# A layer norm, attention and gated feed-forward kernel: GpSimd's column sums in two pieces, a new order at the start, and filler matmuls on TensorE

## The chip, the cores and the metric

The kernel runs on one core of a Trainium2 chip. The metric is the device time of one execution in microseconds (us), the median of the runs. The core's engines are TensorE (PE in the profile, with PEld for its weight loads), VectorE (DVE), ScalarE (ACT), GpSimd (POOL) and SyncE (SP, which here only issues DMAs). They run side by side and wait for one another through semaphores.

## What is computed

The input x is 2048 rows of 256 numbers. It is normalized row by row, goes through causal attention with 16 heads of 128, and the result is multiplied with a gate from a small routed feed-forward layer and added to x:

```python
xn = _layernorm(x)                                   # (x - m) / sqrt(v + 1e-5), x is 2048 x 256
k, q, v = (einsum('ihd,bpd->biph', W, xn) for W in (W_K, W_Q, W_V))   # 16 heads of 128
scores = einsum('biph,biqh->biqp', k, q)             # causal mask, softmax over p with 1/sqrt(128)
z = einsum('biqp,biph->biqh', softmax(masked), v)
s = einsum('df,bqf->bqd', W_O, z_flat)
g = silu(xn @ W_base.T + b_base + 2.0 * routed_lora(xn))   # the best of 8 experts, rank 16
out = x + s * g
```

All products are float32. The kernel makes each from three TensorE passes: every operand is split into a rounded part (hi) and a remainder (lo), and hi*hi, lo*hi and hi*lo are added in PSUM.

## The kernel before

The 2048 rows are four blocks of 512 (b or g = 0 to 3), each of four tiles of 128 rows. The 16 heads are worked off in 8 pairs, and a pair has 80 steps. A step is one tile of keys (128, index kt) against a block of queries (512, index g): a Score (three matmuls), the exponentials, and some steps later a Value (three matmuls, L327 to L329). On the diagonal the tile has only 384, 256 or 128 columns.

What each engine does for a step: ScalarE first writes minus the row maxima into the score bank (the seed, L572 and L574, from `masked` or `maxrow`). TensorE adds the scores to it. ScalarE takes the exponential twice, as `probs` (L603) and rounded as `p_hi` (L604). VectorE makes `p_lo = probs - p_hi` (L662), from two operands in SBUF, and TensorE's Value needs it. GpSimd adds `probs` to `colsum` (L510 for kt = 1, L514 for later kt), one instruction a tile of up to 512 columns; these sums divide the output of a block later. ScalarE waits for the sum of tile n - 3 before it writes the `probs` of tile n + 1. GpSimd also splits weights in hi and lo (L443, L446), masks the row maxima of a diagonal (L472) and, at the start, scales blocks 1 to 3 of x (L484).

A list written by hand sets the order of all jobs: START before the first score, FIRST for pair 0, SCHEDULE for pairs 1 to 6 and LAST for pair 7. Every engine goes through the same list and takes its share of each job. The codes are: m the statistics of a block of x, n its scaling, N its transposes through TensorE (two per block), Pq and Pk the projections (digits: head of the pair, block), V the values' projection, M one tile of a head's row maxima (matmul L841, maximum on VectorE, L709 or with the mask L715), v a Value, Z, S and O the ends of a block, and | the next Score. Jobs that use an auxiliary PSUM bank share three of them in turn; TensorE waits with such a job until VectorE is through with the job three before it.

The start, in the lines that the change touches: SyncE loads x block by block, the first weights in between. VectorE takes statistics (L627, L631), adds EPS (L634), ScalarE takes the square root (L582), VectorE the reciprocal and one Newton step (L642 to L649), and scales block 0 (L655). TensorE fills the three score banks with ones (L788) and then waits for the transposes (L808). Each transposed bank is copied by ScalarE as hi (L588) and VectorE takes lo (L703). SyncE passes the row maxima of a block through DRAM to spread them over all partitions, and ScalarE reorders them into `maxrow` (L557).

## Time and profile before

| | |
|---|---|
| median of 3 runs | 1389.03 us (1389.02 to 1389.19) |
| the profiled execution | 1389.27 us |
| its span, first to last instruction | 1387.4 us |
| PE, PEld busy | 98%, 83% |
| DVE, ACT, POOL busy | 90%, 79%, 64% |
| the chain that ended last | PE 81%, DVE 13%, ACT 3%, issue 2%, POOL 1% |

The profiled execution took 1.9 us more than its span, 0.2 us more than the median. Busy times of engines overlap, so they don't add up to the span. A busy PE is not a PE at its peak: a matmul of 512 columns is shown with some 0.39 us but the next one starts earlier, so the distance between two starts tells more than a duration. The chain is followed back from the last instruction, at each step to what released it.

### The profile page before, as it was taken

To read this page: it belongs to the slowest core of one execution; us is meant where nothing else is said; L and a number is where in the kernel's file an instruction comes from. 1 tells how busy PE (TensorE), PEld (TensorE's weight loads), DVE (VectorE), ACT (ScalarE), POOL (GpSimd) and SP (SyncE) were. 2 spreads that over 40 slices of the span, in tenths; PEclk is the share of its full clock that TensorE was granted. 3 is DMA by queue.
4 is the path that set the end of the run, shared out by engine and by line. 5 is a ranking of instruction groups with operands and counts; after the bars stand their busy time and mean duration, and the time that the engine had idled before them with its cause. 6 is when DMAs were issued, how large, how long until landed. Compare 5 with 4: busy or idle time off the path is not lost.

```text
span 1387.4 us, 23197 instructions
## 1 busy us (share of the span) xinstructions
PE 1355.0 (98%) x7340; PEld 1156.6 (83%) x7340; DVE 1254.3 (90%) x2636; ACT 1100.5 (79%) x2459; POOL 892.7 (64%) x765
## 2 busy tenths in 40 slices
PE   5999999999999999999999999999999999999997
PEld 3788888888788888888888887988888888888987
DVE  6789998999899998989989999899989999889988
ACT  2688887888788897788877888788878889778675
POOL 5456784567566674666745777556766658476566
PEclk9999999999999999999999999999999999999999
DMA  3100001010100101100010000100011000010103
GB/s 99 32 16 16 16 9 46 9 17 16 31 24 9 24 8 32 31 17 8 17 39 17 16 16 8 47 9 17 15 32 24 16 17 9 23 36 16 24 9 107
DMA packets 30137, 33.74 MB, mean 24 GB/s; under 512 B 11072, under 2 KB 17728, under 8 KB 30016
## 3 DMA queue, kind: packets, MB, share of 16 engines
q1 hardware_dynamic: 30016, 32.26, 9.7%
q8 instruction: 59, 0.97, 0.3%
q14 instruction: 62, 0.51, 0.2%
HBM read 30.02 MB, written 2.23 MB: 23 GB/s over the span
## 4 chain that ended last, share of the span: by engine, by line
PE 81%; DVE 13%; ACT 3%; issue 2%; POOL 1%; DMA 0%; ACTq 0%; DVEq 0%
PE ps L327 25%; PE ps L329 24%; PE ps L328 24%; PE ps L841 7%; DVE p_lo L662 5%; DVE partmax L709 3%; PE ps L898 2%; DVE acc L751 1%; DVE z_lo L731 1%; ACT p_hi L604 1%; POOL acc L484 1%; DVE sums L735 1%; ACT ps L574 0%; ACT z_hi L609 0%; ACT probs L603 0%
## 5 line engine op out<-in xcount | busy, mean ns | idle before, releaser
L514 POOL TENSOR_TENSOR colsum<-colsum,probs 128x512 f32<-128x512 f32 (+3 forms) x512 | 640.0, 1250 | 207.9 <-ACT probs L603 176.1
L662 DVE TENSOR_TENSOR p_lo<-probs,p_hi 128x512 fp32r<-128x512 f32 (+3 forms) x640 | 576.3, 905 | 12.8 <-ACT p_hi L604 11.6
L603 ACT ACTIVATE probs<-ps 128x512 f32<-128x512 f32 (+3 forms) x640 | 345.6, 540 | 179.7 <-PE ps L329 174.8
L604 ACT ACTIVATE p_hi<-ps 128x512 fp32r<-128x512 f32 (+3 forms) x640 | 346.3, 541 | 0.0
L574 ACT ACTIVATE ps<-maxrow 128x512 f32<-128x512 f32 (+3 forms) x576 | 315.3, 547 | 0.0
L709 DVE TENSOR_REDUCE partmax<-ps 128x1 f32<-128x512 f32 x384 | 255.5, 679 | 2.7 <-PE ps L841 2.5
L327 PE MATMUL ps<-p_hi,v_hi 128*128 128x512 f32 (+3 forms) x640 | 238.0, 372 | 5.0 <-DVE p_lo L662 3.8
L327 PE MATMUL ps<-qT_hi,kT_hi 128*128 128x512 f32 (+3 forms) x640 | 237.8, 371 | 0.0
L329 PE MATMUL ps<-qT_hi,kT_lo 128*128 128x512 f32 (+3 forms) x640 | 233.0, 364 | 0.0
L328 PE MATMUL ps<-qT_lo,kT_hi 128*128 128x512 f32 (+3 forms) x640 | 232.9, 364 | 0.0
L328 PE MATMUL ps<-p_lo,v_hi 128*128 128x512 f32 (+3 forms) x640 | 232.8, 364 | 0.0
L329 PE MATMUL ps<-p_hi,v_lo 128*128 128x512 f32 (+3 forms) x640 | 232.5, 363 | 0.0
L841 PE MATMUL ps<-kT_hi,qT_hi 128*128 128x512 f32 (+3 forms) x640 | 218.5, 368 | 6.1 <-DVE qT_lo L703 2.6
L510 POOL TENSOR_TENSOR colsum<-probs 128x384 f32<-128x384 f32 (+1 forms) x64 | 79.8, 1247 | 212.2 <-ACT probs L603 212.2
L327 PEld LDWEIGHTS ps<-p_hi,v_hi 128*128 128x128 f32 x640 | 120.4, 188 | 37.5 <-DVE p_lo L662 19.4
L841 PEld LDWEIGHTS ps<-kT_hi,qT_hi 128*128 128x128 f32 x640 | 119.3, 188 | 30.1 <-DVE qT_lo L703 3.5
L327 PEld LDWEIGHTS ps<-qT_hi,kT_hi 128*128 128x128 f32 x640 | 120.6, 188 | 21.5 <-ACT ps L574 6.1
L329 PEld LDWEIGHTS ps<-qT_hi,kT_lo 128*128 128x128 f32 x640 | 120.5, 188 | 19.3
L329 PEld LDWEIGHTS ps<-p_hi,v_lo 128*128 128x128 f32 x640 | 120.4, 188 | 18.8
L328 PEld LDWEIGHTS ps<-p_lo,v_hi 128*128 128x128 f32 x640 | 120.6, 188 | 17.6
L328 PEld LDWEIGHTS ps<-qT_lo,kT_hi 128*128 128x128 f32 x640 | 120.6, 188 | 14.0
L715 DVE CUSTOM_DVE_ANT_0 ps<-ps,mask_rows 128x128 f32<-128x128 f32 (+3 forms) x256 | 124.7, 492 | 0.3
(115 smaller groups left out, 2337.2 us busy)
## 6 DMA issues: line engine op xcount, KB each, us to landing
spread<-max_dram SPq DMA_DIRECT2D x64, 256.0 KB, 3.9
wraw<-wqk_dram SPq DMA_DIRECT2D x16, 256.0 KB, 3.6
acc<-x_dram SPq DMA_DIRECT2D x4, 512.0 KB, 6.3
wraw<-wv_dram SPq DMA_DIRECT2D x8, 256.0 KB, 5.1
wraw<-wo_dram SPq DMA_DIRECT2D x8, 256.0 KB, 3.1
out_dram<-acc SPq DMA_DIRECT2D x8, 256.0 KB, 2.4
max_dram<-rowmax SPq DMA_DIRECT2D x64, 2.0 KB, 1.4
maxrow<-x_dram SPq DMA_DIRECT2D x2, 512.0 KB, 3.8
```

Source lines behind the costliest of these rows:

```text
L327: nc.tensor.matmul(dst, w_hi, m_hi, start=first, stop=False, skip_group_check=seed)
L328: nc.tensor.matmul(dst, w_hi, m_lo, start=False, stop=False, skip_group_check=seed)
L329: return nc.tensor.matmul(dst, w_lo, m_hi, start=False, stop=last, skip_group_check=seed)
L510: nc.gpsimd.tensor_tensor(total[:, c0:], before[:, c0:], tile[:, c0:], ALU.add)\
L514: nc.gpsimd.tensor_tensor(total[:, c0:], total[:, c0:], tile[:, c0:], ALU.add)\
L574: op = nc.scalar.activation(dst[:, plain:], maxrow[:, job.g, plain:], ACT.Copy)
L603: nc.scalar.activation(probs[:, k, c0:], src, ACT.Exp, scale=SCALE).then_inc(probs_ready, 1)
L604: nc.scalar.activation(p_hi[:, k, c0:], src, ACT.Exp, scale=SCALE).then_inc(hi_ready, 1)
L662: nc.vector.tensor_tensor(p_lo[:, k, c0:], probs[:, k, c0:], f32(p_hi[:, k, c0:]), ALU.subtract)\
L709: nc.vector.reduce_max(dst, src, axis=AX).then_inc(aux_free, 1)
L715: nc.vector.tensor_tensor_reduce(out=src[:, 0:w], in0=src[:, 0:w], in1=mask_rows[:, BW - w:], scale=1.0, scalar=-3.0e38, op0=ALU.add, op1= ...
L841: nc.tensor.matmul(dst[:, 0:w], qT_hi[:, job.g, job.q * P:(job.q + 1) * P], kT_hi[:, k_slot(job.head, job.c), 0:w], start=True, stop=True)\
```

## The change

Four things change.

1. GpSimd's sums (L510 and L514) of tiles with 512 or 384 columns are made in two instructions of half the columns. The semaphore rises after the second.
2. The start of the layer norm. Block 0 of x is loaded by two DMAs of two tiles each, and VectorE starts with the first. The addition of EPS (L634) is gone: ScalarE adds it inside the square root, and the Newton step takes the variance with EPS. GpSimd makes `ones_r` first and splits the first weights only when VectorE has scaled block 0. Block 1 is scaled by VectorE instead of GpSimd (`DVE_SCALED = 2`).
3. TensorE no longer waits for all constants before it fills the score banks, and issues matmuls of ones into a bank that is overwritten later: 16 before block 0's transposes, 7 before the first projection, 6 before block 1's transposes, 512 columns each.
4. START and FIRST, up to step 31 of pair 0, have another order. SCHEDULE, LAST and the rest of FIRST stay.

```diff
+                if b == 0:
+                    sp.dma_start(acc[:, 0:2, :], xt[0][:, 0:2]).then_inc(x_in_first, 16)
+                    sp.dma_start(acc[:, 2:TB, :], xt[0][:, 2:TB]).then_inc(x_in[0], 16)
+                    sp.dma_start(wraw[:, 0, :], wqk[:, 0, :]).then_inc(wqk_in, 16)
+                    continue
...
 START = (
-    "m0 n0 m1 n1 N00 N10 m2 Pk00 N01 Pq00 N11 M0020 M0000 M0010 M0030 n2 Pq01 m3 M0110 n3 N02 V01 Pk01 M0130 "
-    "M0111 M0100 M0101 M0120 M0131 "
+    "m0 n0 N00 N10 m1 m2 n1 Pq00 Pk00 N01 n2 M0010 N11 M0030 M0020 M0000 m3 n3 Pq01 V01 Pk01 M0100 N02 N12 M0131 "
+    "M0110 M0120 M0121 M0101 M0111 "
 )
...
+            nc.gpsimd.memset(ones[:, :], 1.0).then_inc(made, 1)
+            nc.gpsimd.memset(eps[:, :], EPS)
+            pool.wait_ge(made, 1)
+            nc.gpsimd.tensor_copy(ones_r[:, :], ones[:, :]).then_inc(ones_ready, 1)
...
+            pool.wait_ge(normed, 4 + TB)
             split_weights(wraw[:, 0, :], flat(wqk_hi[:, 0]), flat(wqk_lo[:, 0]), wqk_in, 16, 1, wqk_ready)
...
-                if isinstance(job, Scale) and job.b:
+                if isinstance(job, Scale) and job.b >= DVE_SCALED:
...
+            def halves(c0):
+
+                middle = (c0 + BW) // 2
+                return (slice(c0, middle), slice(middle, BW)) if c0 < BW - P else (slice(c0, BW),)
...
-                elif job.kt == 1:
-                    before = probs[:, (n - 1) % PROBS, :]
-                    nc.gpsimd.tensor_tensor(total[:, c0:], before[:, c0:], tile[:, c0:], ALU.add)\
-                      .then_inc(sum_done, 2)
                 else:
-                    pool.wait_ge(sum_done, n)
-                    nc.gpsimd.tensor_tensor(total[:, c0:], total[:, c0:], tile[:, c0:], ALU.add)\
-                      .then_inc(sum_done, 1)
+                    other = probs[:, (n - 1) % PROBS, :] if job.kt == 1 else total
+                    if job.kt > 1:
+                        pool.wait_ge(sum_done, n)
+                    for part in halves(c0):
+                        op = nc.gpsimd.tensor_tensor(total[:, part], other[:, part], tile[:, part], ALU.add)
+                    op.then_inc(sum_done, 2 if job.kt == 1 else 1)
...
-                    act.wait_ge(moments_done, job.b + 1)
-                    nc.scalar.activation(rstd[:, 1, mine], rstd[:, 0, mine], ACT.Sqrt).then_inc(sqrt_done, 1)
+                    act.wait_ge(stats_done, 2 * job.b + 2)
+                    nc.scalar.activation(rstd[:, 1, mine], moments[:, mine, 1], ACT.Sqrt, bias=eps[:, 0:1])\
+                      .then_inc(sqrt_done, 1)
...
+            def keep_busy(bank, job):
+
+                first = job.b == 0 if isinstance(job, (Normed, Project)) else False
+                if isinstance(job, Normed) and job.c == 0 and job.b < 2:
+                    times = BUSY_FIRST if first else BUSY_THIRD
+                elif isinstance(job, Project) and first and job.head == 0 and job.which == "q":
+                    times = BUSY_SECOND
+                else:
+                    return
+                for _ in range(times):
+                    nc.tensor.matmul(bank, ones_r[:, :], ones_r[:, None, :].broadcast_to([P, TB, P]), start=True,
+                                     stop=True)
```

The rows below give an engine's instructions in the order of its queue, a line for each or for several alike, with the line number in the kernel they belong to. On TensorE at the start of the program before the change, the first rows are the fill of the score banks, block 0's transposes, a projection (six matmuls), block 1's first transposes:

```order
L788 MATMUL ps<-ones_r 128x128 x12
L808 MATMUL ps<-ident,acc 128x128 x8
L327 MATMUL ps<-xT_hi,wqk_hi 128x512
L328 MATMUL ps<-xT_lo,wqk_hi 128x512
L329 MATMUL ps<-xT_hi,wqk_lo 128x512
L327 MATMUL ps<-xT_hi,wqk_hi 128x512
L328 MATMUL ps<-xT_lo,wqk_hi 128x512
L329 MATMUL ps<-xT_hi,wqk_lo 128x512
L808 MATMUL ps<-ident,acc 128x128 x4
```

The same place after the change:

```order
L805 MATMUL ps<-ones_r 128x128 x12
L821 MATMUL ps<-ones_r 128x512 x16
L841 MATMUL ps<-ident,acc 128x128 x8
L821 MATMUL ps<-ones_r 128x512 x7
L334 MATMUL ps<-xT_hi,wqk_hi 128x512
L335 MATMUL ps<-xT_lo,wqk_hi 128x512
L336 MATMUL ps<-xT_hi,wqk_lo 128x512
...
L821 MATMUL ps<-ones_r 128x512 x6
L841 MATMUL ps<-ident,acc 128x128 x4
L874 MATMUL ps<-kT_hi,qT_hi 128x256
```

Matmuls of ones now stand in three places, and both projections of block 0 (twelve matmuls, nine of them left out) come before block 1's transposes. On VectorE at the start before the change, from block 0's scaling to the first remainders of projections:

```order
L655 TENSOR_SCALAR acc<-acc,moments,rstd 128x256 x4
L627 BN_STATS stats<-acc 128x6 x4
L631 BN_AGGR moments<-stats 128x2 x4
L634 TENSOR_SCALAR rstd<-moments 128x4
L642 RECIPROCAL rstd<-rstd 128x4
L644 TENSOR_TENSOR rstd<-rstd 128x4
L646 SCALAR_TENSOR_TENSOR rstd<-rstd 128x4
L649 SCALAR_TENSOR_TENSOR rstd<-rstd 128x4
L703 TENSOR_TENSOR xT_lo<-ps,xT_hi 128x512 x2
```

The same place after the change:

```order
L673 TENSOR_SCALAR acc<-acc,moments,rstd 128x256 x4
L721 TENSOR_TENSOR xT_lo<-ps,xT_hi 128x512 x2
L648 BN_STATS stats<-acc 128x6 x4
L652 BN_AGGR moments<-stats 128x2 x4
L648 BN_STATS stats<-acc 128x6 x4
L652 BN_AGGR moments<-stats 128x2 x4
L660 RECIPROCAL rstd<-rstd 128x4
L662 SCALAR_TENSOR_TENSOR rstd<-rstd 128x4
L664 SCALAR_TENSOR_TENSOR rstd<-moments,rstd 128x4
L667 SCALAR_TENSOR_TENSOR rstd<-rstd 128x4
L673 TENSOR_SCALAR acc<-acc,moments,rstd 128x256 x4
```

Block 0's transposed remainders (L703, now L721) come right after its scaling, ahead of the statistics of blocks 1 and 2, and block 1's scaling is now here. On GpSimd, in the first steps of pair 0 before the change:

```order
L514 TENSOR_TENSOR colsum<-colsum,probs 128x256
L514 TENSOR_TENSOR colsum<-colsum,probs 128x128
L510 TENSOR_TENSOR colsum<-probs 128x512
L514 TENSOR_TENSOR colsum<-colsum,probs 128x512
L443 TENSOR_TENSOR wo_hi<-wraw,zeros 128x512
L446 TENSOR_TENSOR wo_lo<-wraw,wo_hi 128x512
```

The same place after the change:

```order
L531 TENSOR_TENSOR colsum<-colsum,probs 128x128 x3
L531 TENSOR_TENSOR colsum<-probs 128x256 x2
L531 TENSOR_TENSOR colsum<-colsum,probs 128x256 x2
L453 TENSOR_TENSOR wo_hi<-wraw,zeros 128x512
L456 TENSOR_TENSOR wo_lo<-wraw,wo_hi 128x512
```

A tile of 512 columns is now two instructions of 256 (and one of 256 columns two of 128); the weights' splits are whole as before.

## Rows read from the trace of the kernel before

**Rows 1.** The profile's page, its first line.

```profile
span 1387.4 us, 23197 instructions
```

**Rows 2.** Busy time by stretch: length; PE, PEld, DVE, ACT, POOL busy; PEclk; DMA.

```profile
0.00:60.00 60.00, 40.62 (x181) 31.32 (x182) 42.29 (x126) 25.82 (x54) 27.13 (x43) 0.97 0.22 66
31.50:35.00 3.50, 2.97 (x14) 2.97 (x15) 0.86 (x3) 0.96 (x3) 3.50 (x4) 0.51 0.16 57
60.00:1383.00 1323.00, 1314.33 (x7161) 1125.26 (x7160) 1210.12 (x2509) 1074.70 (x2407) 865.52 (x723) 1.00 0.09 22
```

**Rows 3.** The chain that ended last, its start: start us, us, what.

```profile
6.55 1.25 DVE rstd L634
...
8.87 3.04 DVE acc L655 x4
```

**Rows 4.** Timeline of the start: start us, us, instruction, [idle before <-releaser].

```profile
2.81 2.82 PE L788 MATMUL ps<-ones_r 128*128 128x128 f32 x12 [2.81 <-POOL ones_r L463]
...
16.23 0.76 PE L327 MATMUL ps<-xT_hi,wqk_hi 128*128 128x512 f32 x1 [2.93 <-DVE xT_lo L703]
...
16.79 0.63 PE L328 MATMUL ps<-xT_lo,wqk_hi 128*128 128x512 f32 x1
17.21 0.63 PE L329 MATMUL ps<-xT_hi,wqk_lo 128*128 128x512 f32 x1
...
27.14 9.65 POOL L484 TENSOR_SCALAR acc<-acc,moments,rstd 128x256 f32<-128x256 f32 x8 [7.32 <-DVE rstd L649]
...
38.26 0.64 POOL L472 TENSOR_SCALAR_AFFINE_SELECT gates<-maxrow 128x512 f32<-128x512 f32 x1 [1.47 <-ACT maxrow L557]
...
39.80 0.46 PE L327 MATMUL ps<-qT_hi,kT_hi 128*128 128x512 f32 x1
```

**Rows 5.** Groups of the first 40 us: busy us, mean ns | idle before.

```profile
L627 DVE BATCH_NORM_STATS2 stats<-acc 128x6 f32<-128x256 f32 x16 | 5.6, 410 | 4.7 <-DMA acc<-x_dram 4.7
...
L703 DVE TENSOR_TENSOR xT_lo<-ps,xT_hi 128x512 fp32r<-128x512 f32 x5 | 3.3, 685 | 2.0 <-ACT xT_hi L588 2.0
...
L715 DVE CUSTOM_DVE_ANT_0 ps<-ps,mask_rows 128x128 f32<-128x128 f32 (+3 forms) x6 | 2.6, 459 | 0.0
```

**Rows 6.** Line L655, VectorE's scaling of block 0: ns min/median/max.

```profile
L655 DVE TENSOR_SCALAR acc<-acc,moments,rstd x4: 400/728/1420, 8.9 to 11.5; 128x256 f32<-128x256 f32 x4
```

**Rows 7.** Waits from 60 to 1387 us: us in total, times, longest.

```profile
PEld ps L327 <- DVE p_lo L662: 19.4, 39, 0.8
```

**Rows 8.** Timeline around one such wait, in pair 1.

```profile
309.57 1.30 POOL L514 TENSOR_TENSOR colsum<-colsum,probs 128x512 f32<-128x512 f32 x1 [0.81 <-ACT probs L603]
...
309.71 1.70 DVE L662 TENSOR_TENSOR p_lo<-probs,p_hi 128x512 fp32r<-128x512 f32 x1
...
312.39 1.30 POOL L446 TENSOR_TENSOR wqk_lo<-wraw,wqk_hi 128x512 fp32r<-128x512 f32 x1
...
312.54 1.70 DVE L662 TENSOR_TENSOR p_lo<-probs,p_hi 128x512 fp32r<-128x512 f32 x1
...
313.64 1.74 POOL L514 TENSOR_TENSOR colsum<-colsum,probs 128x512 f32<-128x512 f32 x1
...
313.85 0.34 PE L329 MATMUL ps<-qT_hi,kT_lo 128*128 128x384 f32 x1
...
314.29 0.50 PE L327 MATMUL ps<-p_hi,v_hi 128*128 128x512 f32 x1
...
314.63 0.40 PE L328 MATMUL ps<-p_lo,v_hi 128*128 128x512 f32 x1
...
314.86 0.40 PE L329 MATMUL ps<-p_hi,v_lo 128*128 128x512 f32 x1
```

**Rows 9.** Groups by shape, 60 to 1387 us, `p_lo` of full tiles: busy, mean.

```profile
L662 DVE TENSOR_TENSOR p_lo<-probs,p_hi 128x512 fp32r<-128x512 f32 x445 | 462.8, 1042 | 12.4 <-ACT p_hi L604 11.6
```

**Rows 10.** Timeline: a sum of 256 columns, and a `p_lo` beside an idle GpSimd.

```profile
49.27 0.73 POOL L514 TENSOR_TENSOR colsum<-colsum,probs 128x256 f32<-128x256 f32 x1
...
300.11 0.66 DVE L662 TENSOR_TENSOR p_lo<-probs,p_hi 128x512 fp32r<-128x512 f32 x1
```

More of the change, by code:

```diff
@@ L38 @@
 X_FIRST = 56
+DVE_SCALED = 2
+BUSY_FIRST, BUSY_SECOND, BUSY_THIRD = 16, 7, 6
 LORA_STEP = 49
@@ L237, in attention_layer @@
         rank = sb("rank", [P, TB, E])
+        eps = sb("eps", [P, 1])
         warm = sb("warm", [P, 2])
@@ L315, in attention_layer, with normed_until @@
         assert mask_at == sorted(mask_at) and max_blocks == sorted(max_blocks)
+        def normed_until(b):
+            return 4 * b + TB * min(b, DVE_SCALED)
         def columns(t):
@@ L449, in flat @@
                 return t.rearrange("p a b -> p (a b)") if len(t.shape) == 3 else t.rearrange("p a b c -> p (a b c)")
+            nc.gpsimd.memset(ones[:, :], 1.0).then_inc(made, 1)
+            nc.gpsimd.memset(eps[:, :], EPS)
+            pool.wait_ge(made, 1)
+            nc.gpsimd.tensor_copy(ones_r[:, :], ones[:, :]).then_inc(ones_ready, 1)
             nc.gpsimd.memset(ident[:, :], 0.0).then_inc(made, 1)
             nc.gpsimd.memset(mask_rows[:, :], 0.0).then_inc(made, 1)
-            nc.gpsimd.memset(zeros[:, :], 0.0)
-            nc.gpsimd.memset(ones[:, :], 1.0).then_inc(made, 1)
+            nc.gpsimd.memset(zeros[:, :], 0.0).then_inc(made, 1)
             for e in range(E):
                 nc.gpsimd.memset(rank[:, :, e:e + 1], float(E - e))
-            pool.wait_ge(made, 3)
+            pool.wait_ge(made, 4)
             diagonal = dict(compare_op=ALU.not_equal, base=0, pattern=[[-1, P]], channel_multiplier=1)
@@ L461, in _ @@
             nc.gpsimd.affine_select(out=mask_rows[:, BW - P:], in_=mask_rows[:, BW - P:], compare_op=ALU.is_ge,
-                                    fill=MASKED, base=0, pattern=[[-1, P]], channel_multiplier=1)
-            nc.gpsimd.tensor_copy(ones_r[:, :], ones[:, :]).then_inc(consts, 1)
+                                    fill=MASKED, base=0, pattern=[[-1, P]], channel_multiplier=1).then_inc(consts, 1)
+            pool.wait_ge(normed, 4 + TB)
             split_weights(wraw[:, 0, :], flat(wqk_hi[:, 0]), flat(wqk_lo[:, 0]), wqk_in, 16, 1, wqk_ready)
@@ L632, in block_moments @@
                 op.then_inc(stats_done, 1)
-                dve.wait_ge(stats_done, 2 * b + 2)
-                nc.vector.tensor_scalar(rstd[:, 0, TB * b:TB * (b + 1)], moments[:, TB * b:TB * (b + 1), 1], EPS, None,
-                                        ALU.add).then_inc(moments_done, 1)
             def scale_block(b):
-                mine, done = slice(TB * b, TB * (b + 1)), TB * (b > 0) + 4 * b
-                r, v = rstd[:, 2, mine], rstd[:, 0, mine]
+                mine, done = slice(TB * b, TB * (b + 1)), normed_until(b)
+                r, v = rstd[:, 2, mine], moments[:, mine, 1]
                 dve.wait_ge(sqrt_done, b + 1)
@@ L643, in scale_block @@
                 dve.wait_ge(normed, done + 1)
-                nc.vector.tensor_tensor(rstd[:, 3, mine], r, r, ALU.mult).then_inc(normed, 1)
+                nc.vector.scalar_tensor_tensor(rstd[:, 3, mine], r, -0.5, r, ALU.mult, ALU.mult).then_inc(normed, 1)
                 dve.wait_ge(normed, done + 2)
-                nc.vector.scalar_tensor_tensor(rstd[:, 4, mine], rstd[:, 3, mine], -0.5, v, ALU.mult, ALU.mult)\
+                nc.vector.scalar_tensor_tensor(rstd[:, 4, mine], v, EPS, rstd[:, 3, mine], ALU.add, ALU.mult)\
                   .then_inc(normed, 1)
@@ L650, in scale_block @@
                   .then_inc(normed, 1)
-                if b:
+                if b >= DVE_SCALED:
                     return
                 dve.wait_ge(normed, done + 4)
-                for t in range(TB):
+                for t in range(TB * b, TB * (b + 1)):
                     nc.vector.tensor_scalar(acc[:, t, :], acc[:, t, :], moments[:, t, 0:1], rstd[:, 5, t:t + 1],
@@ L782, in _ @@
         def _(pe):
-            pe.wait_ge(consts, 1)
+            pe.wait_ge(ones_ready, 1)
             for bank in st:
@@ L800, in _ @@
                         pe.wait_ge(aux_free, job.aux - AUX_BANKS + 1)
+                    keep_busy(dst, job)
+                    if job.aux == 0:
+                        pe.wait_ge(consts, 1)
                 if isinstance(job, Normed):
@@ L803, in _ @@
                         tok = TB * job.b + t
-                        if job.b == 0:
-                            pe.wait_ge(normed, 4 + t + 1)
+                        if job.b < DVE_SCALED:
+                            pe.wait_ge(normed, normed_until(job.b) + 4 + t + 1)
                         else:
-                            pe.wait_ge(scaled, TB * (job.b - 1) + t + 1)
+                            pe.wait_ge(scaled, TB * (job.b - DVE_SCALED) + t + 1)
                         op = nc.tensor.transpose(dst[:, t * P:(t + 1) * P],
```

15 lines of the change are left out of this document (8 added, 7 removed), and 20 rows, old and new, of the table FIRST.

## The prediction, made before the changed kernel ran

> **What bounds the kernel now.** I read the span first, then the engines by stretch, then the chain and the waits. The span is 1387.4 us [rows 1]. From 60 us to 1383 us TensorE is busy 1314 of 1323 us, VectorE 1210 of them and GpSimd 866; in the first 60 us TensorE is busy only 40.6 [rows 2]. The TensorE work of the whole program doesn't change except for the ones, so a gain can come from three places only: the 19.4 us without a matmul in the first 60 us, the time there at half clock, and the small holes in the dense part.
>
> *The start.* Block 0's statistics begin when x has landed, at 4.7 us [rows 5]. The EPS addition on 4 columns takes 1.25 us and the scaling of four tiles 3.04 us, done at 11.9 [rows 3], though a tile takes 0.40 us when nothing is in its way [rows 6]. The first projection starts at 16.23 and the first score at 39.80 [rows 4]. Ahead of the score GpSimd scales blocks 2 and 3, eight tiles in 9.65 us from 27.14 on, then masks the maxima (38.26), and 1.54 us after the mask's start the score runs [rows 4].
>
> *The clock.* Projections of 512 columns start 0.42 us apart at 17 us [rows 4], which is TensorE's lower level (1.2 GHz); at 314 us it is 0.23 us, near the upper one [rows 8]. Between 31.5 and 35 us, after stretches of waiting, the granted clock is 0.51 [rows 2].
>
> *The dense part.* TensorE waits for `p_lo` 39 times [rows 7]. One such wait: the matmul before it has 384 columns and starts at 313.85, the next one at 314.29, 0.44 us later instead of about 0.17 (384/512 of 0.23); the one behind starts 0.34 us later instead of 0.23 [rows 8]. That is 0.38 us lost. Why `p_lo` is late is in the same rows: GpSimd adds a tile from 309.57 to 310.87, and the `p_lo` that starts at 309.71 takes 1.70 us and ends at 311.41, 0.54 us after GpSimd. Beside an idle GpSimd it takes 0.66 us [rows 10]; the mean is 1.04 us over 445 [rows 9]. So VectorE waits for the end of GpSimd's instruction, and that costs it (1.04 - 0.66) x 445 = 169 us in all.
>
> By the Trainium skill, page "SBUF — State Buffer", section "SBUF: two separate sides", VectorE with two SBUF inputs and GpSimd share a port pair that is locked for a whole instruction, and the loser blocks fully. The trace agrees: 0.54 us after GpSimd's end.
>
> **The change, part by part.**
>
> *Block 0's norm (sum's first term).* The EPS addition goes (1.25 us). With the weights' split behind the scaling, four tiles cost 0.40 + 3 x 0.32 = 1.4 us instead of 3.04 (0.32 being what a tile adds in the queue; I work it out from the four statistics, 5.6/4 = 1.4 us a block [rows 5], which run alike). The first half of x lets two of the four statistics run early; the same bytes have to land for the second half, so I take 0.7 us, half of the 1.4 (bounds 0 and 1.4). 11.9 - 1.25 - 1.6 - 0.7 = 8.3 us. The square root with a bias I take like the one without. Then ScalarE's copy (0.6 us, as VectorE's of 0.685 [rows 5]) and the remainders of two banks, 2 x 0.64: block 0 is in place at about 10.8. The split of the first weights, now from 8.3 on, takes at most 2 x 1.3 us (both halves like that of [rows 8]) and ends by 10.9, level with it. First projection at 10.8 instead of 16.2: **5.4 us**.
>
> *The ones.* The fill takes 2.82 us from 2.81 on [rows 4] and moves ahead by some 1.3 us, since only one memset and one copy stand before it. So 16 matmuls start near 4.3: at 0.42 us they end at 11.0, at 0.23 us at 8.0. The tiles are scaled from 7.3 on. When the clock rises is the open point: between 31.5 and 35 us it was down for the whole 3.5 us with 2.97 us of work in them [rows 2], and came back at the end. The same from 1.5 us on gives 5, and the ones end near 8.4. The transposes then take 0.15 us each at full clock and the evacuation is about in time: cost 0 to 0.5 us. The groups of 7 and 6 (1.6 and 1.4 us at full clock) lie in waits for `xT_lo` and for block 1's scaling; without that cover they would cost 3 us together. Their return is that the projections, 24 matmuls before the first score, run at 0.23 us instead of 0.42, partly off the path.
>
> *From the first projection to the first score.* After, VectorE sets the pace up to block 3's numbers: three blocks' statistics and small operations (3 x 2.6 us; 2.6 is what block 0 needs from 4.7 to 8.87 without the 1.25 and ScalarE's turn of 0.3), the scaling of block 1 (1.4), four remainders (2.8), four masked maxima (4 x (0.46 + 0.14) = 2.4) and a row maximum, 0.2: 14.6 us, from 10.8 to 25.4, with small gaps 25.8. GpSimd gets block 2 at about 19.7 and is through at 24.5, waits, takes block 3 in half of 9.65 us: 30.6. Then mask and seed, 1.54: first score at 32.2. TensorE's own list of auxiliary jobs comes to 32.5, by VectorE's maxima. That is 39.8 - 32.5 = **7.3 us** for the start as a whole (the 5.4 included), and one transposed bank more is done by then (4 transposes, 0.5 us). Block 1's scaling costs GpSimd 4.8 us less and VectorE 1.4 more. I keep 7.5, with 4 and 10 as bounds: 4 if the ones run to 11 us, 10 if the first steps of pair 0 close their holes too.
>
> *GpSimd's pieces.* A sum of 256 columns takes 0.73 us [rows 10], so a tile takes 1.46 instead of 1.30: some 400 tiles x 0.16 = 64 us more for GpSimd, which has 457 us idle in the dense part [rows 2]. That hides it; without this cover the path would carry it. A `p_lo` that asks during the first piece now waits for 0.73 us at most, and saves 1.30 - 0.73 = 0.57 us; 0.73/1.30 = 56% of those that meet a sum do. Some of the blockers are splits and masks, which stay whole (the second `p_lo` of [rows 8] waits for one). I expect 0.18 us off the mean of 1.04, 80 us less for VectorE. For TensorE the lateness counts: 39 waits x 0.38 = 15 us, and each hole is smaller than the 0.57 us of a single saving. With three in four gone that is **11 us**; bounds 0 (other work of VectorE sets the wait) and 19 (all of them, and the waits for maxima behind the same queue).
>
> Does VectorE get in between two pieces at all? They are issued back to back. [rows 8] show it: GpSimd's sum has started at 313.64, before its split's end at 313.69, yet the waiting `p_lo` ends at 314.24 and the sum takes 1.74. So the waiting engine comes next.
>
> **Sum.** 1389.0 - 7.5 - 11 = **1370.5 us** for the median (the profiled execution is 0.2 us above it, its span 1.9 below).
>
> **The rivals.**
>
> *A: the pieces bring nothing.* The waits have another cause: the 39 are set by VectorE's total (1210 of 1323 us), and SCHEDULE, made for whole sums, finds new places to wait. For it: [rows 8], where the last blocker is a split. Against: VectorE's total itself falls. 1381.5 us.
>
> *B: the start brings little.* The ones run at half clock until 11 us, or the aux banks hold TensorE up, and pair 0 gives back. Gain 1 to 4 there: 1375 to 1379 us.
>
> *C, the other side: GpSimd falls behind.* Between its pieces it is blocked by `p_lo` (0.54 us): a tile costs 0.73 + 0.54 + 0.73 = 2.0 us, and a step lasts (1383 - 60)/620 = 2.1 us. With splits of 2.6 us in between, the sum of tile n - 3 comes late, ScalarE holds the exponential, TensorE the score. It decides from the point where GpSimd's work per step passes 2.1 us for longer than three steps. Price: 2 us a pair for 8 pairs and no gain of 11, 1389 - 7.5 + 16 = 1397.5 us. Against it: 457 us of idle time [rows 2], and that only about half of the tiles can block both ways.
>
> *D: GpSimd keeps the port pair over both pieces*, which would make a `p_lo` wait 1.46 us; 39 holes of 0.16 more, 1388 us. [rows 8] speak against it, though with a split and a sum, not two pieces.
>
> **How the numbers follow.** Both gains as worked out 0.70, A 0.12, B 0.09, C 0.05, D 0.04. Lower end: start 10 and pieces 17 give 1362; upper end: A, at 1382. What a measurement here can tell from no change is 0.2%, 2.8 us, so faster means below 1386.2. Faster 0.91 (the first three), same 0.04 (D), slower 0.05 (C).
>
> **What would show it.** First projection near 10.8 us and first score near 32.5; a granted clock of 1.00 from about 7 us to the end of the dense part; `p_lo` of 512 columns with a mean near 0.86 us; fewer than 15 waits of TensorE for `p_lo`; GpSimd's busy time near 960 to 1050 us. C would show as waits of ScalarE's `probs` for the sums, A as the same 39 waits at a shorter `p_lo`, D as `p_lo` of up to 2.0 us. The prediction fails if the pieces meet fewer `p_lo` than I think, or if the start's new order leaves TensorE waiting behind the first scores.

## The result, and the profile after

| | before | after |
|---|---|---|
| median | 1389.11 us (1389.02 to 1389.51, 4 runs) | 1380.99 us (1380.36 to 1381.24, 4 runs) |
| span of the profiled execution | 1387.4 us | 1379.1 us |

The ratio is 0.9936 with a 95% interval of 0.9924 to 0.9949 (the two medians of the table divide to 0.9942, inside it). The kernel is 8.1 us faster; 18.5 were forecast. The time lies 0.8% above the forecast.

The profile's page of the changed kernel, its first lines (answers to the busy times in the table ahead):

```profile
span 1379.1 us, 23750 instructions
PE 1358.0 (98%) x7369; PEld 1164.6 (84%) x7369; DVE 1180.9 (86%) x2636; ACT 1100.0 (80%) x2459; POOL 1011.0 (73%) x1274
```

GpSimd's 1011 us lie in the forecast 960 to 1050, but they are 118 more than before (893 us), where the prediction's sum had 64. The sums of full tiles before (60 to 1387 us), and then their pieces after (60 to 1379 us), tell why:

```profile
L514 POOL TENSOR_TENSOR colsum<-colsum,probs 128x512 f32<-128x512 f32 x336 | 502.9, 1497 | 150.4 <-ACT probs L603 130.7 <-POOL colsum L514 0.4
```

```profile
L531 POOL TENSOR_TENSOR colsum<-colsum,probs 128x256 f32<-128x256 f32 x669 | 592.1, 905 | 84.4 <-ACT probs L621 55.0 <-POOL colsum L531 0.9
```

A tile took 1.50 us on average and takes 1.81, two pieces of 905 ns: 0.31 us more, where the durations of an undisturbed GpSimd (0.73 and 1.30 us) gave 0.16. Each piece is lengthened by 0.17 us, nearly as much as a whole sum by its 0.20. The `p_lo` of 512 columns alone, in the same groups with the forms apart (60 to 1370 us), answers to [rows 9]:

```profile
L680 DVE TENSOR_TENSOR p_lo<-probs,p_hi 128x512 fp32r<-128x512 f32 x444 | 391.7, 885 | 23.1 <-ACT p_hi L622 22.8
```

1042 ns became 885. And the waits of 60 to 1379 us (in total, times, longest), which answer to [rows 7]:

```profile
PEld ps L334 <- DVE p_lo L680: 11.4, 23, 1.3
...
ACT ps L589 <- POOL gates L485: 3.1, 1, 3.1
PE ps L334 <- ACT ps L591: 2.8, 1, 2.8
```

TensorE's weight loads wait 23 times for `p_lo` instead of 39, 11.4 us instead of 19.4. The last two lines are new: one wait of ScalarE for a mask of GpSimd, and behind it one of TensorE for the seed. Windows of the same trace, to be read beside [rows 2] (behind the five engines stand PEclk, the DMA share and GB/s):

```profile
0.00:60.00 60.00, 54.45 (x252) 43.49 (x253) 43.49 (x136) 30.63 (x64) 27.62 (x48) 0.91 0.23 67
19.90:26.70 6.80, 6.56 (x21) 5.33 (x22) 5.03 (x24) 2.43 (x5) 6.11 (x6) 0.50 0.13 39
60.00:1375.00 1315.00, 1303.52 (x7119) 1121.15 (x7117) 1135.89 (x2499) 1069.35 (x2396) 983.37 (x1227) 1.00 0.09 22
204.20:207.60 3.40, 3.40 (x16) 3.40 (x15) 0.00 (x0) 1.45 (x4) 0.46 (x1) 0.50 0.69 168
```

The clock is at its lower level (0.50, 1.2 GHz) for 6.8 us from 19.9 on, for 3.4 us from 33.5 on, and again for 3.4 us at 204, right behind the new wait. The start, from the timeline, one row for each landmark:

```profile
3.44 1.40 DVE L648 BATCH_NORM_STATS2 stats<-acc 128x6 f32<-128x256 f32 x4 [3.44 <-DMA acc<-x_dram]
...
6.42 1.39 DVE L673 TENSOR_SCALAR acc<-acc,moments,rstd 128x256 f32<-128x256 f32 x4
...
3.96 4.93 PE L821 MATMUL ps<-ones_r 128*128 128x512 f32 x16
...
11.43 0.47 PE L334 MATMUL ps<-xT_hi,wqk_hi 128*128 128x512 f32 x1
...
22.04 0.63 PE L336 MATMUL ps<-xT_hi,wqk_lo 128*128 128x512 f32 x1
22.46 0.63 PE L334 MATMUL ps<-xT_hi,wqk_hi 128*128 128x512 f32 x1
...
24.88 4.82 POOL L502 TENSOR_SCALAR acc<-acc,moments,rstd 128x256 f32<-128x256 f32 x4 [0.69 <-DVE rstd L667]
31.90 0.64 POOL L485 TENSOR_SCALAR_AFFINE_SELECT gates<-maxrow 128x512 f32<-128x512 f32 x1 [2.20 <-ACT maxrow L574]
...
33.61 0.63 PE L334 MATMUL ps<-qT_hi,kT_hi 128*128 128x512 f32 x1
...
35.13 0.60 ACT L621 ACTIVATE probs<-ps 128x512 f32<-128x512 f32 x1 [1.27 <-PE ps L336]
```

The first score starts at 33.61 instead of 39.80 [rows 4], 6.2 us earlier. The first exponential starts at 35.13 instead of 40.75, only 5.6 earlier, because this score runs at the lower clock (0.63 us a matmul, as the rows at 22 us, which are 0.42 us apart).

**Where the rest went.** The first exponential of a pair is a mark that every trace has, since a pair is 80 steps in all kernels here. For pair 2, before and then after:

```profile
373.71 0.60 ACT L603 ACTIVATE probs<-ps 128x512 f32<-128x512 f32 x1 [0.22 <-PE ps L329]
...
538.42 0.60 ACT L603 ACTIVATE probs<-ps 128x512 f32<-128x512 f32 x1 [0.22 <-PE ps L329]
```

```profile
369.13 0.60 ACT L621 ACTIVATE probs<-ps 128x512 f32<-128x512 f32 x1 [0.21 <-PE ps L336]
...
532.24 0.60 ACT L621 ACTIVATE probs<-ps 128x512 f32<-128x512 f32 x1 [0.21 <-PE ps L336]
```

Pair 2 took 164.71 us and takes 163.11. I read all pairs so, from the timeline of each kernel's trace (us; the last pair goes to the end of the span):

| kernel | first exp. | 0 | 1 | 2 | 3 | 4 | 5 | 6 | 7 | after first exp. |
|---|---|---|---|---|---|---|---|---|---|---|
| before | 40.8 | 168.0 | 165.0 | 164.7 | 164.8 | 164.7 | 162.5 | 164.8 | 192.3 | 1346.7 |
| after | 35.1 | 169.3 | 164.8 | 163.1 | 163.1 | 163.2 | 163.2 | 163.1 | 194.2 | 1343.9 |
| e1_pieces | 40.8 | 170.2 | 164.4 | 163.2 | 163.2 | 163.2 | 163.1 | 163.2 | 194.5 | 1344.9 |
| e2_start | 33.7 | 166.3 | 164.9 | 164.7 | 164.6 | 164.7 | 164.7 | 164.6 | 192.4 | 1347.0 |
| e6_one_mask | 35.6 | 165.7 | 163.3 | 163.2 | 163.2 | 163.3 | 163.2 | 163.1 | 194.3 | 1339.4 |
| e8_both | 35.1 | 166.0 | 163.3 | 163.2 | 163.2 | 163.3 | 163.2 | 163.2 | 192.4 | 1337.9 |
| e12_splits | 33.9 | 165.2 | 162.9 | 162.7 | 162.8 | 162.9 | 162.7 | 162.7 | 191.8 | 1333.6 |

After against before: 5.6 us from the first exponential, 1.6 in each of pairs 2, 3, 4 and 6, 0.3 in pair 1; against that 1.3 lost in pair 0, 0.7 in pair 5 and 1.9 in pair 7. Together that is 8.4 us, the difference of the spans but for rounding.

**The hole in pair 0.** GpSimd, then ScalarE, then TensorE in the timeline near the end of pair 0:

```profile
186.64 15.27 POOL L531 TENSOR_TENSOR colsum<-colsum,probs 128x256 f32<-128x256 f32 x16
201.87 0.63 POOL L485 TENSOR_SCALAR_AFFINE_SELECT gates<-maxrow 128x512 f32<-128x512 f32 x1
...
197.10 1.15 ACT L574 ACTIVATE maxrow<-spread 128x512 f32<-128x512 f32 x1
...
202.62 0.28 ACT L589 ACTIVATE ps<-gates 128x128 f32<-128x128 f32 x1 [3.09 <-POOL gates L485]
...
200.15 0.40 PE L874 MATMUL ps<-kT_hi,qT_hi 128*128 128x512 f32 x1
203.36 0.50 PE L334 MATMUL ps<-qT_hi,kT_hi 128*128 128x512 f32 x1 [2.81 <-ACT ps L591]
```

and ScalarE and GpSimd in the same place before:

```profile
204.38 1.15 ACT L557 ACTIVATE maxrow<-spread 128x512 f32<-128x512 f32 x1
...
191.91 13.76 POOL L514 TENSOR_TENSOR colsum<-colsum,probs 128x512 f32<-128x512 f32 x8
205.67 0.64 POOL L472 TENSOR_SCALAR_AFFINE_SELECT gates<-maxrow 128x512 f32<-128x512 f32 x1
```

The maxima are ready at 198.25 (197.10 + 1.15), but the mask stands behind eight tiles of sums that GpSimd works off without a gap, and starts at 201.87. Eight tiles take 15.27 us in pieces and took 13.76 whole, 1.91 against 1.72 each.

Only half of the lateness of 3.6 us comes from GpSimd. Counted from the first exponential, the mask starts 1.8 us later than before (166.74 against 164.92 us): 1.5 from these eight tiles and 0.3 from those before them. The maxima are ready 1.7 us earlier (163.12 against 164.78), since the rest of pair 0 got shorter. And before there was no slack: the maxima were ready at 205.53 and the mask started at 205.67. So GpSimd had to keep pace with a faster chain, and became slower. The steps are shorter there than the average of 2.1 us, as ScalarE's exponentials of the first and the last of the eight tiles show:

```profile
183.89 0.63 ACT L621 ACTIVATE probs<-ps 128x512 f32<-128x512 f32 x1
...
196.14 0.49 ACT L621 ACTIVATE probs<-ps 128x384 f32<-128x384 f32 x1 [0.45 <-PE ps L336]
```

That is 1.75 us a step for sums of 1.91; before it was 1.82 (190.70 to 203.42) for sums of 1.72. The seed waits, TensorE stands for 2.81 us, and the clock drops behind it for 3.4 us, in which TensorE does half of what it could: some 1.7 us more, by that estimate.

### The profile page after: what moved, and what is told of

Its sections match the earlier page's. It is cut to its first block, busy times and chain, and to the rows that moved or that the text cites. A ratio compares the mean times of both kernels' runs of the same rounds, so it can differ in the third digit from the quotient of the medians.

```text
span 1379.1 us, 23750 instructions
## 1 busy us (share of the span) xinstructions
PE 1358.0 (98%) x7369; PEld 1164.6 (84%) x7369; DVE 1180.9 (86%) x2636; ACT 1100.0 (80%) x2459; POOL 1011.0 (73%) x1274
## 4 chain that ended last, share of the span: by engine, by line
PE 84%; DVE 9%; POOL 3%; ACT 1%; issue 1%; POOLq 0%; DVEq 0%; ACTq 0%
PE ps L334 25%; PE ps L336 24%; PE ps L335 24%; PE ps L874 8%; DVE p_lo L680 3%; POOL colsum L531 3%; DVE partmax L727 2%; PE ps L931 2%; DVE v_lo L721 1%; DVE z_lo L749 1%; DVE sums L753 0%; ACT v_hi L606 0%; PE ps L821 0%; ACT p_hi L622 0%; ACT ps L591 0%
## 5 line engine op out<-in xcount | busy, mean ns | idle before, releaser
L531 POOL TENSOR_TENSOR colsum<-colsum,probs 128x256 f32<-128x256 f32 (+2 forms) x960 | 751.2, 801 | 126.3 <-ACT probs L621 79.5
L680 DVE TENSOR_TENSOR p_lo<-probs,p_hi 128x512 fp32r<-128x512 f32 (+3 forms) x640 | 499.3, 784 | 25.8 <-ACT p_hi L622 25.2
L531 POOL TENSOR_TENSOR colsum<-probs 128x256 f32<-128x256 f32 (+1 forms) x128 | 100.8, 809 | 184.8 <-ACT probs L621 184.8
L334 PEld LDWEIGHTS ps<-p_hi,v_hi 128*128 128x128 f32 x640 | 120.5, 188 | 29.6 <-DVE p_lo L680 11.4
```

The costliest lines, as they stand in the source:

```text
L334: nc.tensor.matmul(dst, w_hi, m_hi, start=first, stop=False, skip_group_check=seed)
L531: op = nc.gpsimd.tensor_tensor(total[:, part], other[:, part], tile[:, part], ALU.add)
L680: nc.vector.tensor_tensor(p_lo[:, k, c0:], probs[:, k, c0:], f32(p_hi[:, k, c0:]), ALU.subtract)\
```

## The experiments

Each kernel is compared with the kernel before on the same chip. e1 to e4 ran together, then e5 to e8, then e9 to e12; the kernel before took 1388.52, 1388.54 and 1389.69 us beside them. All compute everything that the changed kernel computes.

**e1_pieces**: the kernel before, with GpSimd's two pieces alone.

```diff
...
+                    for part in halves(c0):
+                        op = nc.gpsimd.tensor_tensor(total[:, part], other[:, part], tile[:, part], ALU.add)
+                    op.then_inc(sum_done, 2 if job.kt == 1 else 1)
```

As in the changed kernel, `halves` makes two pieces of a tile of 256 columns too, and leaves only those of 128 whole.

> The kernel before with GpSimd's sums in two pieces and nothing else of the change. Theory 1 (the pieces shorten TensorE's waits for p_lo by some 1.6 us a pair in six of eight pairs, and lose part of it again where GpSimd's queue falls behind, above all at the last steps of pair 0, where a mask stands behind a row of sums): 1389.1 - 6 x 1.65 + a hole of 1 to 5 us, 1380 to 1384 us, and a wait of ScalarE for the mask near 210 us. Rival A (the pieces bring nothing, all of the gain is the start's): 1388 to 1390 us. The changed kernel itself is 1381.0.

Measured: 1387.05 us, ratio 0.9988 (0.9978 to 0.9998). Alone the pieces bring next to nothing in the total, yet its pairs 2 to 4 and 6 take 163.2 us as in the changed kernel. The hole is there too, with the same 3.1 us, in the waits and in GpSimd's timeline:

```profile
ACT ps L576 <- POOL gates L472: 3.1, 1, 3.1
...
192.96 15.28 POOL L518 TENSOR_TENSOR colsum<-colsum,probs 128x256 f32<-128x256 f32 x16
208.19 0.63 POOL L472 TENSOR_SCALAR_AFFINE_SELECT gates<-maxrow 128x512 f32<-128x512 f32 x1
```

So the hole comes with the pieces and not with the new start. Pair 0 is 2.2 us longer than before, and pair 7 too.

**e2_start**: the changed kernel with whole sums.

```diff
-                return (slice(c0, middle), slice(middle, BW)) if c0 < BW - P else (slice(c0, BW),)
+                return (slice(c0, BW),)
```

> The changed kernel with GpSimd's sums whole again, so only the start, the ones and the new order. Theory 1: the start is worth 5.6 to 7 us at step 72 of pair 0, and without the pieces there is no late mask: 1382 to 1383.5 us, first exponential at 35.1 us, TensorE's waits for p_lo again near 39. Rival A: 1381 us, like the changed kernel. Rival B (the start brings little): above 1386 us.

Measured: 1384.41 us, ratio 0.9969 (0.9958 to 0.998). That is 4.1 us less than the kernel before took beside it. The first exponential starts at 33.7, 1.4 us before the changed kernel's; but the profiled execution, at 1382.67 us, is the fastest of the seven. There is no hole at the end of pair 0, and the waits for `p_lo` are back (60 to 1380 us):

```profile
PEld ps L334 <- DVE p_lo L680: 21.9, 44, 0.8
```

The clock was at its lower level for one stretch only, 3.4 us from 21.0 on. A window in it:

```profile
21.10:24.30 3.20, 2.91 (x8) 2.17 (x8) 3.02 (x17) 0.08 (x1) 3.20 (x4) 0.50 0.02 1
```

Up to the first score the program is the same in both, so the start's gain varies with where the clock falls. Pair 5 takes 164.7 us here, with whole sums, like its neighbours.

**e3_mask**: every mask two steps earlier in GpSimd's queue.

```diff
-            mask_at.append(max(order_at[block], diagonal - MASK_AHEAD))
+            mask_at.append(max(order_at[block] - 2, diagonal - MASK_AHEAD))
```

> The changed kernel, but where the mask's place in GpSimd's queue is set by ScalarE's reordering of the maxima, it stands two sums earlier. Theory 1 (the 3.2 us hole at 200 us, and the half clock of some 3.4 us behind it, come from the mask queued behind sums that are late): the hole goes, 5 us less, 1375 to 1377 us, and the granted clock stays at 1.00 at 204 us. Rival (the hole comes from the maxima's way through DRAM or from ScalarE, and the mask's place is of no matter): 1380.5 to 1381.5 us, with the hole where it was.

Measured: 1394.7 us, ratio 1.0043 (1.0028 to 1.0058): slower than before. The hole of pair 0 is gone (165.3 us), but pairs 2, 3, 5 and 6 take 166.8. Its waits from 60 us on show why:

```profile
POOL gates L485 <- ACT maxrow L574: 41.9, 20, 3.9
PE ps L931 <- POOL colsum L531: 13.1, 7, 2.2
```

GpSimd now stands at masks whose maxima aren't there (41.9 us instead of the changed kernel's 8.9), and TensorE waits seven times for the last sum of a block. Behind four of these waits, at 458, 625, 956 and 1124 us, the granted clock is at its lower level for 3.4 us; they lie in the four pairs of 166.8 us, while pairs 1 and 4 take 165.5 and 165.3. A queue in order takes a step that comes too early as badly as one too late.

**e4_order**: the changed kernel with START and FIRST of before.

```diff
-    "m0 n0 N00 N10 m1 m2 n1 Pq00 Pk00 N01 n2 M0010 N11 M0030 M0020 M0000 m3 n3 Pq01 V01 Pk01 M0100 N02 N12 M0131 "
+    "m0 n0 m1 n1 N00 N10 m2 Pk00 N01 Pq00 N11 M0020 M0000 M0010 M0030 n2 Pq01 m3 M0110 n3 N02 V01 Pk01 M0130 "
...
```

> The changed kernel with START and FIRST of the kernel before (pieces, ones, and the new layer norm stay). If the new order carries the start's gain: 1386 us or more, with the first score near 38 us. If the faster layer norm alone carries it: 1381 to 1383 us, with the first score near 36 us. The late mask at the end of pair 0 depends on how far GpSimd is behind there, and should stay, since the last steps of pair 0 are the same in both orders.

Measured: 1389.55 us, ratio 1.0005 (0.9996 to 1.0014). The first exponential starts at 43.4, later than before. The first projection, in the timeline:

```profile
15.42 0.76 PE L334 MATMUL ps<-xT_hi,wqk_hi 128*128 128x512 f32 x1 [4.54 <-DVE xT_lo L721]
```

In the old order VectorE does block 1's statistics and scaling (m1, n1) before it takes block 0's remainders, and TensorE stands 4.5 us; and blocks 2 and 3 are again scaled in one row of eight tiles, from 28.4 to 38.0. The faster layer norm brought nothing in this order. Why the first exponential is even 2.6 us later isn't settled: the granted clock is lower from 32.5 to 39.3 us and from 42.7 on, where the kernel before has one such stretch, from 31.6 to 35.0.

**e5_no_ones**: the changed kernel without the matmuls of ones.

```diff
-BUSY_FIRST, BUSY_SECOND, BUSY_THIRD = 16, 7, 6
+BUSY_FIRST, BUSY_SECOND, BUSY_THIRD = 0, 0, 0
```

> The changed kernel without the 29 matmuls of ones. Theory 1 (they lie in TensorE's waits and only keep its clock up): the projections and transposes before the first score run at 0.43 us a matmul of 512 columns up to about 15 us, first exponential 1 to 3 us later, 1382 to 1384 us. If they only delay: 1379 to 1381 us. If they make no difference: 1381 us.

Measured: 1378.88 us, ratio 0.993 (0.9916 to 0.9945), the same as with them. In the timeline its first projections stand 0.43 us apart, at the lower clock, where the changed kernel's run at the upper one, but they start earlier:

```profile
10.73 0.76 PE L334 MATMUL ps<-xT_hi,wqk_hi 128*128 128x512 f32 x1 [1.50 <-DVE xT_lo L721]
11.29 0.63 PE L335 MATMUL ps<-xT_lo,wqk_hi 128*128 128x512 f32 x1
11.72 0.63 PE L336 MATMUL ps<-xT_hi,wqk_lo 128*128 128x512 f32 x1
```

The granted clock reads 1.00 in the profile here (a window from 11 to 16 us), which 0.43 us a matmul doesn't fit; at the start I go by the distance. 10.73 against 11.43: here the ones cost 0.7 us and give back as much. The first exponential starts at 34.7 instead of 35.1. But 11.43 is near the best of the traces with ones and the new order, in which the first projection starts between 11.39 (e8) and 12.77 us (e6); without ones it is 10.73 and 10.74 (e9). So the ones cost 0.7 to 2.0 us.

**e6_one_mask**: one mask alone two steps earlier, the one of the hole.

```diff
-            mask_at.append(max(order_at[block], diagonal - MASK_AHEAD))
+            mask_at.append(max(order_at[block] - 2 * (gi == 2 * NB), diagonal - MASK_AHEAD))
```

> The changed kernel with the mask two sums earlier at one place only, the first block of pair 1, whose mask is the one that came 3.1 us late at 200 us. In the last round the earlier mask at every block mended pair 0 (165.3 us from its first exponential to pair 1's instead of 169.3) but made pairs 2 to 7 longer (166.8 us instead of 163.1), with TensorE waiting for sums. Theory 1 (a single late mask costs 4 us in pair 0 and 1.6 us of half clock in pair 1, and nothing else is wrong): pair 0 165.3, pair 1 163.1, pairs 2 to 6 163.1 each; ratio to the changed kernel's own time 0.996, so about 0.990 of the kernel before. Rival (the hole moves to the next mask or sum): no less than the changed kernel, 0.993 to 0.994.

Measured: 1376.89 us, ratio 0.9909 (0.9892 to 0.9925). GpSimd in the same place:

```profile
186.66 11.73 POOL L531 TENSOR_TENSOR colsum<-colsum,probs 128x256 f32<-128x256 f32 x12
198.41 0.64 POOL L485 TENSOR_SCALAR_AFFINE_SELECT gates<-maxrow 128x512 f32<-128x512 f32 x1
```

The mask starts at 198.41, when the maxima are just ready (198.27 here), the clock stays up there, pair 0 takes 165.7 instead of 169.3 and pair 1 163.3 instead of 164.8. This one place had cost 4.9 us.

**e8_both**: e6, and whole sums in pair 7.

```diff
...
-                return (slice(c0, middle), slice(middle, BW)) if c0 < BW - P else (slice(c0, BW),)
+                return (slice(c0, middle), slice(middle, BW)) if c0 < BW - P and n < (PAIRS - 1) * TILES else (slice(c0, BW),)
...
```

> As the one with a single earlier mask, and in pair 7 the sums are whole again. With pieces pair 7 took 194.2 us from its first exponential to the end, with whole sums 192.4. Theory 1 (each loss is GpSimd's queue being late, at known places): 1.8 us below the kernel with the single earlier mask, 0.9885 of the kernel before. If pair 7's loss is not GpSimd's queue but something of the start: no difference between the two.

Measured: 1374.94 us, ratio 0.9897 (0.9882 to 0.9912). The intervals of e6 and e8 overlap, so the totals alone don't tell them apart, but pair 7 takes 192.4 as before, instead of 194.3. In it the output's work comes on top for GpSimd, which is busy for 139 us of it in the changed kernel and for 126 of the pairs before it. So the pieces cause the loss. Where it arises is known in part only: TensorE stands 0.4 us for a split of the weights that e8 doesn't wait for, and 1.1 us for the last `p_lo` instead of 0.6.

**e7_quarters**: four pieces of 128 columns.

```diff
-                middle = (c0 + BW) // 2
-                return (slice(c0, middle), slice(middle, BW)) if c0 < BW - P else (slice(c0, BW),)
+                return [slice(c, c + P) for c in range(c0, BW, P)]
```

> The changed kernel with every sum in pieces of 128 columns (four for a full tile). Theory 1 (p_lo waits for the end of one GpSimd instruction, and GpSimd pays a fixed part and a blocking for each piece): mean p_lo of full tiles falls from 0.88 to about 0.75 us, a tile costs GpSimd 4 x 0.46 = 1.84 us plus blocking, about the 2.04 us of a step, so it falls behind: TensorE and ScalarE wait for sums and masks, pairs of 166 us or more, 1400 us or more in all. If the fixed part of a piece can be hidden: pairs of 162 to 163 us.

Measured: 1436.57 us, one run. Now GpSimd keeps up in no pair: all take 170 us or more. The waits for it in the dense part:

```profile
ACT probs L620 <- POOL colsum L530: 53.6, 59, 2.1
ACT ps L588 <- POOL gates L485: 27.8, 13, 5.3
```

This is rival C as it was written: ScalarE's `probs` wait for the sums 59 times.

**e9_both_no_ones**: e8 without the ones.

```diff
-BUSY_FIRST, BUSY_SECOND, BUSY_THIRD = 16, 7, 6
+BUSY_FIRST, BUSY_SECOND, BUSY_THIRD = 0, 0, 0
```

> The best kernel so far (the change, one earlier mask, whole sums in pair 7) without the matmuls of ones. In the last round the first exponential came at 34.7 us without ones and at 35.1 to 35.6 with them, so I expect no difference that can be measured: 0.9885 to 0.990 of the kernel before. If the ones do pay in most executions, and that profile was a lucky one: 0.991 to 0.992.

Measured: 1373.12 us, ratio 0.9885 (0.987 to 0.99), against e8's 0.9897: again no effect of the ones that can be told apart.

**e10_old_start**: e1 with the two mends of e8, so the pieces without the start.

```diff
...
-                return (slice(c0, middle), slice(middle, BW)) if c0 < BW - P else (slice(c0, BW),)
+                return (slice(c0, middle), slice(middle, BW)) if c0 < BW - P and n < (PAIRS - 1) * TILES else (slice(c0, BW),)
...
-            mask_at.append(max(order_at[block], diagonal - MASK_AHEAD))
+            mask_at.append(max(order_at[block] - 2 * (gi == 2 * NB), diagonal - MASK_AHEAD))
```

> The kernel before with only the sums in pieces in pairs 0 to 6, one earlier mask and whole sums in pair 7: the steady part alone, with the old start. Theory 1 (pieces are worth 1.6 us in each of pairs 1, 2, 3, 4 and 6 and as much or a little more in pair 0, once their backlog is mended; nothing in pairs 5 and 7): first exponential at 40.8, 1389 - 9.5 = 1379.5 us, 0.993 of the kernel before. If the pieces need the new start: 0.996 or more.

Measured: 1380.9 us, ratio 0.9935 (0.9923 to 0.9948). Its first exponential starts at 38.7, and from there to the end it takes 1337.9 us, 8.8 less than before. e8 takes the same 1337.9. So mended pieces are worth 8.8 us, and that adds to the start's gain.

The first exponential at 38.7 is 2.1 us earlier than in the kernel before, though all code up to it is the same. The first projection starts at 14.19 instead of 16.23. VectorE's timeline has the reason:

```profile
6.42 0.17 DVE L638 TENSOR_SCALAR rstd<-moments 128x4 f32<-128x4 f32 x1
...
8.16 1.38 DVE L659 TENSOR_SCALAR acc<-acc,moments,rstd 128x256 f32<-128x256 f32 x4
```

The EPS addition takes 0.17 us instead of 1.25 and the scaling 1.38 instead of 3.04 [rows 3]. Here both start ahead of GpSimd's next split of weights (at 6.45 and 9.27 us); in the kernel before they start just behind it (6.50 and 8.73). Which comes first differs between traces of the same code (in e1 the addition takes 1.25 us, as in the kernel before), so part of what the new start takes away is lost in some executions only.

**e12_splits**: e8, and the weights' splits in two pieces each too.

```diff
...
+                for part in parts:
+                    op = nc.gpsimd.tensor_tensor(hi[:, part], raw[:, part], zeros[:, 0:1].broadcast_to([P, w]), ALU.add)
+                op.then_inc(weight_hi, 1)
...
+                for part in parts:
+                    op = nc.gpsimd.tensor_tensor(lo[:, part], raw[:, part], f32(hi[:, part]), ALU.subtract)
+                op.then_inc(ready, 1)
```

> The best kernel so far with the weights' splits on GpSimd in two pieces each as well. Theory 1 (what is left of TensorE's waits for p_lo comes behind whole splits): four splits a pair, each p_lo of 1.8 us behind one falls to about 1.2, pairs 1 to 6 fall from 163.2 to 162.5 us, 0.5% ahead at most 4 us in all: 0.986 to 0.989 of the kernel before. If GpSimd's added time costs as much: pairs of 163.2 us or more, 0.990 or more.

Measured: 1370.13 us, ratio 0.9865 (0.9852 to 0.9878), the fastest version of all, 1.35% below the kernel before. Every pair is 0.3 to 0.8 us shorter than e8's, with fewer waits for `p_lo` (e8: 11.2 us, 24 times):

```profile
PEld ps L334 <- DVE p_lo L685: 7.4, 18, 0.8
```

**e11_again**: the changed kernel once more, with no edit.

> The changed kernel itself, to stand beside the others of this call on one chip: 0.9936 of the kernel before again (interval before 0.9924 to 0.9949), first exponential at 34 to 35.5 us by where the clock falls, the late mask at 200 us again.

Measured: 1380.93 us, ratio 0.9935 (0.9922 to 0.9947). The result stands, and e9, e10 and e12 can be read against it, as they ran beside it.

## Why the prediction was too high in its gain

**Block 0's norm: right.** The first half of x let the statistics start at 3.44. The square root takes 0.30 us with its bias, the scaling 1.39 (1.4 forecast), and it ended at 7.81 against 8.3. The first projection came at 11.43 against 10.8, so the 5.4 us measured 4.8. The ones ended at 8.9, and transposes and remainders followed from there; the terms as the prediction writes them out add up to 10.2 and hold no transposes. The 16.2 it counts from is not firm either, as e10 shows with 14.2.

**First projection to first score: 0.5 us too good**, which with those 0.6 makes the first score 1.1 us late (33.6 against 32.5). Block 2 was scaled from 19.36 on (19.7 forecast), block 3 done at 29.70 (30.6 forecast): VectorE's and GpSimd's shares were right. What failed is "a granted clock of 1.00 from about 7 us": from 19.9 to 26.7 and from 33.5 on it was 0.50. Six projections and twelve matmuls of V ran there, and everything behind them came later: the mask stood 2.20 us for the maxima. The start term of 7.5 us measured 5.6 here. In all kernels with this start and order the first exponential came between 32.4 (e9) and 35.6 (e6), and the granted clock goes with it: 32.4 where it never fell once it had risen, 33.7 to 33.9 in the four with one low stretch ahead of it (e2, e3, e7, e12), 34.7 to 35.6 in the five with a second one from about 33 us on. With the old start it came between 38.7 (e10) and 40.8, so the start gives 3.1 to 8.4 us. By medians it gives 4.1 alone (e2) and 4.8 beside mended pieces (13.6 in e8, 8.8 in e10). When the clock falls there stays open, and it differs between executions of one kernel (19.9 us in the changed kernel's trace, 22.3 in e11's).

**The ones: cost 0.7 to 2.0 instead of 0 to 0.5, and no return in total.** They raised the clock before the first projection, and delayed it; the ratios are 0.9936 with them and 0.993 without (e5), 0.9897 and 0.9885 (e8, e9). The forecast had the lower level end with them, and no new one begin.

**The pieces in the regular pairs: right in mechanism, near in size.** 11 us over 8 pairs is 1.4 a pair; pairs 2, 3, 4 and 6 gave 1.6. VectorE fell by 74 us in the dense part (1210 of 1323 us to 1136 of 1315; 80 forecast), `p_lo` to 885 ns (860). The count of waits was wrong: 23 instead of fewer than 15, with less than half of the lost time gone. e12 shows what sets part of the rest: GpSimd's splits, which stayed whole. Pair 5 gave nothing, as it had taken 162.5 us before already. That is not a property of whole sums, since it takes 164.7 in e2; why it was short in that trace is open.

**The step that failed** is "which has 457 us idle in the dense part [rows 2]. That hides it". It is a sum over 1323 us. At the end of pair 0 GpSimd has no gap for eight tiles, and each took 0.19 us more, while the maxima came 1.7 us earlier. So the mask behind them, which had been just in time, was late by 3.6 us. That, the clock behind it and the loss in pair 7 took 4.9 + 1.9 us (e6 and e8 show both by mending them), so that the term of 11 us gave 2.8 in the changed kernel (1346.7 - 1343.9) and 1.8 in e1. What was to be hidden was mis-sized as well: a tile costs GpSimd 0.31 us more, not 0.16, since a piece is lengthened nearly as much as a whole sum. Of the 10.5 us by which the time missed the forecast, 8.2 are the pieces' and 1.9 the start's; the other 0.4 lie between medians and spans.

**The rivals.** C's mechanism was right, its form was not: it was written as a lateness in every pair, looked for at `probs`, and given 0.05. It struck in pair 0, through a mask, and by e8 in pair 7. It also compared GpSimd's work with the mean step of 2.1 us; a tile of 1.91 us is below that, and the queue fell behind all the same, because the steps there last 1.75 us. "For longer than three steps" was the right kind of mark, but I did not look for such a stretch, though the trace of before shows it (eight tiles in 13.76 us without a gap, the mask behind them). A gives 1381.5, 0.5 us from the measured time, by a cause that the runs refute: the regular pairs are 1.6 us shorter in e1, with nothing but the pieces in it. That the sum fits a rival is no evidence for it. B, the start bringing little, is true in part: 5.6 us of 7.5 here, above the 1 to 4 that it gave. D is refuted: no `p_lo` took 2.0 us. The longest of all took 1.80, and it began as a split of 1.29 us did, so two pieces are not held as one.

## What to carry to other kernels

Before an instruction is made dearer on an engine that works in order, look for the longest stretch in which that engine has no gap, for what others wait for behind it, and how long the steps are just there; its idle time in total tells nothing of that. When a total comes out smaller than the parts promise, compare equal stretches of the two traces: gains of 1.6 us a pair and two losses were both plain there, and the mends were one number and one condition. A step of a queue is moved alone: moving all masks cost some 14 us against the changed kernel, moving one gained 4. And a start of 40 us varies from one execution to the next by 2 us and more, so its gain isn't read from one trace.
